# Causal attention: small masked tiles joined two to a PSUM bank, with a new order of jobs

## The chip, the cores and the metric

One core of one Trainium2 chip runs the kernel. The metric is the device time of one execution in microseconds (us); where several executions were timed, their median. Engines are named as in the profile: PE (TensorE matmuls), PEld (its weight loads), DVE (VectorE), ACT (ScalarE), POOL (GpSimd), SP (the DMA issuing queue).

## The reference

Two transformer layers on x of shape 4 x 1024 x 128, all in f32. Each layer normalises, attends with 16 heads of 8 dimensions, adds, normalises, applies a gated feed-forward network of 384 hidden units and adds. The second layer's attention is causal, and its projection weights are 8 times larger, so its scores spread widely and the softmax needs a true row maximum.

```python
logits = jnp.einsum('bshd,bkhd->bhsk', q, k) / np.sqrt(hd)
mask = k_pos > q_pos
logits = jnp.where(mask[None, None, :, :], -jnp.inf, logits)
attn = jax.nn.softmax(logits, axis=-1)
out = jnp.einsum('bhsk,bkhd->bshd', attn, v).reshape(b, s, d)
return out @ W_out + b_out
```

## The kernel before

A **window** is one sequence and four heads, so each layer has 16 windows. A window's queries fall into two halves of 512 (f = 0 or 1), each half into four blocks of 128 (qb).

For every window the kernel runs two passes over the scores. The first finds the row maxima. It is cut into **jobs**: one matmul of 128 queries against up to 512 keys into one PSUM bank (L1100), which DVE then reduces to a column of maxima, by a plain reduction where no key is masked (L882) and by a reduction with a mask added where the tile touches the diagonal (L879). In the causal layer a window has 48 tiles: 16 whole ones of 512 columns, and 32 masked ones, eight each of 128, 256, 384 and 512 columns. Before the change each tile is one job. Jobs take turns in a ring of three banks (`job_ring=3`): PE waits on `ring_free` before it writes a bank (L1095), DVE waits on `ring_full` before it reads one (L876).

When all jobs of a half are reduced, DVE negates the maxima (L888), POOL splits them in two bf16 parts (L536, L538), PE transposes them (L1150, the *shift* unit), ACT copies them and SP sends them by DMA into two spare rows of the query operand (L430). The second pass can then compute scores with the maximum already subtracted: a *scores* unit (L1132) holds two heads of one block of 128 keys, with up to 512 queries each, plus four small matmuls that add the mask on the diagonal (L1140). ACT takes the exponential (L653), a *sums* block on PE multiplies by the values (L1166), and at a half's end a *norm* unit transposes the sums (L1028). Scores units share a ring of two.

Heads 0 and 2 use array rows 0 to 63, heads 1 and 3 rows 64 to 127 (L1099, L1131), so that neighbouring matmuls of heads of different parity can run side by side. Sums blocks and shift units use 32-column tiles of the array instead.

Every engine walks one list, `Plan.walk` (L99 to L131), written as a string `order` for one **turn**: j is a job, s a scores unit, p a sums block, H and h shift units, N and n norm units. Turn t issues the scores and sums of window t; its jobs are those of later windows, `jobs_ahead` jobs further on. With 59 jobs ahead and 48 per window, the first scores of window 0 come after all 48 jobs of window 0 and 11 of window 1, and in turn 14 only 37 jobs are left. The list `tiles` gives the jobs' sequence within a window; a token such as `321` is head 3, block 2, key half 1. Each engine's program is in order, so a wait holds everything behind it.

The first jobs of the causal layer are issued during the end of the previous layer: 18 on PE (L1246, L1251, L1266, L1273) and 22 on DVE (L969, L984, L995), between the last feed-forward and projection work. DVE's `split_parts` there (L813) leads to the stores to DRAM and to the load of window 1's operands by SP (L421), which window 1's first job waits for (L1098).

Of the kernel before, what the change touches and what calls it, by code (L numbers as in the profile page):

```python
# [13 lines left out]
P = 128  # L14
# [36 lines left out]
class Plan:  # L51
# [12 lines left out]
    def __init__(self, causal, heads, unit_ring, job_ring, alternate, order, jobs_ahead, sums_behind, project_at, wide_step=99, tiles=None):  # L64
# [15 lines left out]
        for f in range(2):  # L80
            for qb in range(TPC):
                width = (TPC * f + qb + 1) * P if causal else S
                in_head_order = [(c, kh) for r in range(PAIRS) for kh in range(2) for c in (2 * r, 2 * r + 1)] if alternate \
                    else [(c, kh) for c in range(HG) for kh in range(2)]
                for c, kh in in_head_order:
                    w = min(width - kh * CHUNK, CHUNK)
                    if w > 0:
                        stream.append((f, c, qb, kh, w, causal and kh * CHUNK + w == width))
        if tiles:
            found = {x[:4]: x for x in stream}  # L90
            stream = [found.pop((f, *(int(d) for d in token))) for f in range(2) for token in tiles[f].split()]
            assert not found
        self.first_job = stream[0]
        self.last_of_half = [[x for x in stream if x[0] == f][-1] for f in range(2)]
# [53 lines left out]
    def ends_half(self, job):  # L148
# [8 lines left out]
              order="jjHjsjjsjjjspjssjjpjsjjsjspjjssjjpsjjpjssjjpjsjjsjpsjjjspjjssjjpjjsjspjjjhnNjjsjpjjssjjp",  # L157
              jobs_ahead=59, sums_behind=1, project_at=(4, 6, 10),
              tiles=("120 110 030 130 020 320 330 100 230 010 220 300 000 310 210 200",
                     "310 121 311 100 030 300 211 200 321 031 201 230 110 231 120 210 221 330 021 001 320 010 301 331 111 000 101 011 131 220 130 020"))]  # L160
# [7 lines left out]
def transformer_pair_kernel(nc, x_in, wqkv_a, bqkv_a, wout_a, bout_a, wqkv_b, bqkv_b, wout_b, bout_b,  # L168
# [10 lines left out]
    with ExitStack() as ctx:  # L179
# [590 lines left out]
        def _(dve):  # L770
# [95 lines left out]
            def run_job(layer, job, number):  # L866

                plan, job_base = PLANS[layer], layer * PLANS[0].jobs_all
                f, c, qb, kh, width, diagonal = job
                if number in plan.paired:  # L870
                    if kh == 0:
                        run_pair(plan, f, c, qb, number // 4 * 2 + c % 2)
                    return
                slot = number % plan.job_ring
                src, dst = psum[:, plan.job_bank + slot, 0:width], maxima[:, f, c, qb, kh:kh + 1]
                dve.wait_ge(ring_full, job_base + number + 1)  # L876
                if diagonal:
                    dve.sem_inc(begun, 1)
                    nc.vector.tensor_tensor_reduce(out=junk[:, slot, 0:width], in0=src, in1=mask[:, CHUNK - width:], scale=1.0,  # L879
                                                   scalar=LOWEST, op0=ALU.add, op1=ALU.max, accum_out=dst).then_inc(ring_free, 1)  # L880
                else:
                    nc.vector.tensor_reduce(dst, src, AX_X, ALU.max).then_inc(ring_free, 1)  # L882
# [8 lines left out]
            def jobs_and_negations(layer, items):  # L891

                for kind, w, number, what in items:
# [6 lines left out]
                    if kind == "job" and PLANS[layer].ends_half(what):  # L900
                        unnegated.append((what[0], number + 1))
# [103 lines left out]
        def _(pe):  # L1005
# [79 lines left out]
            def run_job(layer, w, job, number):  # L1085

                plan, job_base = PLANS[layer], layer * PLANS[0].jobs_all
                f, c, qb, kh, width, _ = job
                if number in plan.paired:
                    if number % 4 == 0:  # L1090
                        two_pairs(plan, f, c, qb, number // 2)
                    return
# [3 lines left out]
                if job == plan.first_job:  # L1096
                    earlier = layer * len(range(buf, WINDOWS, BUFS))
                    pe.wait_ge(operands_loaded[buf], (w // BUFS + earlier + 1) * LOADS)  # L1098
                rows, r = slice(TILE_ROWS * (c % 2), TILE_ROWS * (c % 2) + JOB_ROWS), c // 2  # L1099
                mm(psum[:, bank, 0:width], qop[rows, buf, f, r, qb * P:(qb + 1) * P].bitcast(F32R),  # L1100
                   kop[rows, buf, r, kh * CHUNK:kh * CHUNK + width].bitcast(F32R), start=True, stop=True).then_inc(ring_full, 1)
# [215 lines left out]
```

## Time and profile before

| what | value |
| --- | --- |
| median of 3 runs | 1334.71 us (1332.62 to 1335.34) |
| profiled execution | 1338.29 us, span 1336.4 us |
| mean granted clock of PE | 0.968 of full |
| causal attention, first to last exponential | 839.14 to 1270.41 us |
| one steady turn | 26.8 us |

The span runs from the first to the last instruction of the profiled execution; the execution's own time holds some 2 us besides. A matmul's recorded end is modelled and includes the time its result takes to leave the array, so PE looks busy almost throughout; the distance from one start to the next tells more. A turn begins with the exponential of its first scores unit.

### The profile page before, as it was taken

To read this page: it belongs to the slowest core of one execution; us is meant where nothing else is said; L and a number is where in the kernel's file an instruction comes from. 1 tells how busy PE (TensorE), PEld (TensorE's weight loads), DVE (VectorE), ACT (ScalarE), POOL (GpSimd) and SP (SyncE) were. 2 spreads that over 40 slices of the span, in tenths; PEclk is the share of its full clock that TensorE was granted. 3 is DMA by queue.
4 is the path that set the end of the run, shared out by engine and by line. 5 is a ranking of instruction groups with operands and counts; after the bars stand their busy time and mean duration, and the time that the engine had idled before them with its cause. 6 is when DMAs were issued, how large, how long until landed. Compare 5 with 4: busy or idle time off the path is not lost.

```text
span 1336.4 us, 26857 instructions
## 1 busy us (share of the span) xinstructions
PE 1290.7 (97%) x9681; PEld 656.2 (49%) x9681; DVE 1176.7 (88%) x2979; ACT 1004.5 (75%) x1791; POOL 142.1 (11%) x309
## 2 busy tenths in 40 slices
PE   8899999999999999999988987999999999999998
PEld 6434343433434443434335764555555555555487
DVE  7699999999999999999926988799899999999276
ACT  8678888888888888888884531677777777777753
POOL 5630000000000000000002211200000000000011
PEclk9689999999999999999999996799999999999999
DMA  7611001111101111100000433112111211120001
GB/s 209 204 33 34 21 14 34 33 33 34 32 8 29 34 33 33 33 23 13 2 1 1 122 99 95 34 39 59 36 35 38 59 37 34 35 64 4 3 25 40
DMA packets 40060, 58.44 MB, mean 44 GB/s; under 512 B 7796, under 2 KB 19448, under 8 KB 39928
## 3 DMA queue, kind: packets, MB, share of 16 engines
q1 hardware_dynamic: 39928, 56.72, 17.7%
q8 instruction: 77, 1.26, 0.4%
q14 instruction: 55, 0.45, 0.1%
HBM read 36.77 MB, written 18.87 MB: 42 GB/s over the span
## 4 chain that ended last, share of the span: by engine, by line
PE 88%; DVE 5%; ACT 3%; issue 2%; DMA 1%; SPq 0%; POOL 0%; DVEq 0%; ACTq 0%; POOLq 0%
PE psum L1166 30%; PE psum L1132 21%; PE psum L1100 21%; PE psum L1253 4%; PE psum L1028 3%; PE psum L1237 2%; ACT probs L653 2%; PE psum L1140 2%; PE psum L1039 1%; DVE maxima L882 1%; DVE hid L958 1%; PE psum L1182 1%; PE psum L1077 1%; PE psum L1013 1%; PE psum L1150 1%
## 5 line engine op out<-in xcount | busy, mean ns | idle before, releaser
L653 ACT ACTIVATE probs<-psum 128x512 f32<-128x512 f32 (+3 forms) x1386 | 821.8, 669 | 153.0 <-PE psum L1132 83.0
L882 DVE TENSOR_REDUCE maxima<-psum 128x1 f32<-128x512 f32 x1232 | 767.8, 682 | 8.6 <-PE psum L1100 6.6
L1100 PE MATMUL psum<-kop,qop 62*128 62x512 f32 (+2 forms) x1744 | 519.4, 429 | 7.0 <-DVE maxima L879 3.1
L1132 PE MATMUL psum<-qop,kop 64*128 64x512 f32 (+3 forms) x1792 | 514.2, 427 | 9.2 <-ACT probs L653 7.9
L1166 PE MATMUL psum<-probs,v 128*32 128x512 f32 (+3 forms) x3584 | 440.5, 564 | 0.7 <-ACT sums L660 0.7
L1100 PEld LDWEIGHTS psum<-kop,qop 62*128 62x128 f32 x1744 | 266.4, 189 | 203.4 <-DVE maxima L882 119.3
L1132 PEld LDWEIGHTS psum<-qop,kop 64*128 64x128 f32 x1792 | 247.5, 187 | 232.1 <-ACT probs L653 205.9
L879 DVE CUSTOM_DVE_ANT_0 junk<-psum,mask 128x512 bf16<-128x512 f32 (+3 forms) x512 | 232.6, 487 | 38.7 <-PE psum L1100 34.9
L1166 PEld LDWEIGHTS psum<-probs,v 128*32 128x32 f32 x3584 | 71.1, 108 | 120.0 <-issue 89.2
L546 POOL TENSOR_TENSOR att<-att_raw,rden 128x128 f32<-128x128 f32 x64 | 26.1, 409 | 536.9 <-DVE rden L911 536.9
L1140 PE MATMUL psum<-half_ident,key_mask 64*128 64x64 bf16 x1024 | 74.3, 197 | 0.0
L536 POOL TENSOR_TENSOR shift<-negmax,zeros 128x16 bf16<-128x16 f32 x64 | 14.2, 223 | 470.9 <-DVE negmax L888 462.5
L669 ACT CAST shift_rows<-psum 32x128 f32<-32x128 bf16 x64 | 16.5, 258 | 56.2 <-PE psum L1150 56.2
L1237 PE MATMUL psum<-ffn_xt,gate_up_w 128*128 128x512 f32 x192 | 52.6, 409 | 6.0 <-DVE hid L958 5.9
L793 DVE TENSOR_TENSOR x<-psum,x 128x512 f32<-128x512 f32 x32 | 22.1, 690 | 39.7 <-PE psum L1182 26.4
L1253 PE MATMUL psum<-down_w,hid 128*128 128x128 f32 x384 | 48.1, 282 | 4.8 <-DVE hid L958 4.7
L1140 PEld LDWEIGHTS psum<-half_ident,key_mask 64*128 64x128 bf16 x1024 | 43.2, 96 | 18.4 <-issue 6.5
L745 ACT ACTIVATE hid<-psum 128x512 f32<-128x512 f32 x48 | 28.5, 598 | 30.3 <-PE psum L1237 29.9
L1253 PEld LDWEIGHTS psum<-down_w,hid 128*128 128x128 f32 x384 | 45.3, 196 | 7.7 <-DVE hid L958 7.1
L620 ACT ACTIVATE qk<-psum,bqk 128x512 f32<-128x512 f32 x32 | 21.1, 684 | 32.8 <-PE psum L1039 32.6
L879 DVE DVE_READ_ACCUMULATOR2_ANT maxima<- 128x1 f32 x512 | 42.5, 83 | 0.0
L1028 PE MATMUL psum<-ident,sums 128*128 128x128 f32 x256 | 38.7, 283 | 2.4 <-ACT sums L660 1.6
(102 smaller groups left out, 750.4 us busy)
## 6 DMA issues: line engine op xcount, KB each, us to landing
qop<-q_parts SPq DMA_DIRECT2D x256, 64.0 KB
kop<-k_parts SPq DMA_DIRECT2D x64, 128.0 KB
kop<-k_parts SPq DMA_DIRECT2D x128, 64.0 KB
q_parts<-parts SPq DMA_DIRECT2D x24, 256.0 KB, 2.9
k_parts<-parts SPq DMA_DIRECT2D x24, 256.0 KB, 3.2
x<-in_L_attn_a_x SPq DMA_DIRECT2D x8, 256.0 KB, 4.6
q_parts<-att SPq DMA_DIRECT2D x8, 256.0 KB, 3.7
k_parts<-att SPq DMA_DIRECT2D x8, 256.0 KB, 3.8
```

Of the source, the lines that this page charges most:

```text
L546: nc.gpsimd.tensor_tensor(dst, att_raw[:, f, :, :, 0:HD], rden[:, f].rearrange("p t (h o) -> p t h o", o=1).broadcast_to([P, TPC, HG, HD]) ...
L653: nc.scalar.activation(probs[:, slot, heads[0] % 2:heads[-1] % 2 + 1, c0:], psum[:, bank:bank + len(heads), c0:], ACT.Exp, scale=SCORE_SCA ...
L745: nc.scalar.activation(hid[:, c, :], psum[:, 2 + 2 * (c % 2), :], ACT.Silu, scale=DEQUANT).then_inc(silu_ready, 1)
L879: nc.vector.tensor_tensor_reduce(out=junk[:, slot, 0:width], in0=src, in1=mask[:, CHUNK - width:], scale=1.0, scalar=LOWEST, op0=ALU.add, ...
L882: nc.vector.tensor_reduce(dst, src, AX_X, ALU.max).then_inc(ring_free, 1)
L1028: ins = nc.tensor.transpose(psum[:, bank, t * P:(t + 1) * P], src[:, t, :], ident[:])
L1100: mm(psum[:, bank, 0:width], qop[rows, buf, f, r, qb * P:(qb + 1) * P].bitcast(F32R), kop[rows, buf, r, kh * CHUNK:kh * CHUNK + width].bit ...
L1132: ins = mm(psum[:, bank + k, c0:], kop[rows, buf, c // 2, j * P:(j + 1) * P].bitcast(F32R), qop[rows, buf, f, c // 2, c0:].bitcast(F32R), ...
L1140: ins = mm(psum[:, bank + k, at:at + TILE_ROWS], key_mask[rows, part, :], half_ident[rows], start=False, stop=part == 1)
L1166: ins = mm(psum[32 * c:32 * c + 32, 7, c0:], v[:, at:at + 32], probs[:, slot, c % 2, c0:], start=(j == 0), stop=(s == plan.half_end[f]), t ...
L1237: ins = mm(psum[:, 2 + 2 * (c % 2) + k, :], gate_up_w[:, k, c, :].bitcast(F32R), ffn_xt[:, part].bitcast(F32R), start=part == 0, stop=part ...
L1253: ins = mm(psum[:, 7, t * P:(t + 1) * P], hid[:, c, t * P:(t + 1) * P], down_w[:, c, :], start=(c == 0), stop=(c == FB - 1))
```

## The change

A list token may now join tiles with a plus, and each entry of the list is one job of one or two tiles. The joined tiles are 128 with 384 columns or 256 with 256, so a job never exceeds one bank; their heads have the same parity. PE writes both tiles one behind the other into one bank and signals once; DVE waits once, reduces each tile with its own instruction as before and frees the bank once. Of the 48 tiles of a window 24 are joined, so that it has 36 jobs. The order of the turn, the tile list and the number of jobs ahead (59 to 37) are new. The counts of jobs issued early stay at 18 and 22.

```diff
--- before.py
+++ after.py
@@ -86,12 +86,15 @@
                     w = min(width - kh * CHUNK, CHUNK)
                     if w > 0:
                         stream.append((f, c, qb, kh, w, causal and kh * CHUNK + w == width))
+        stream = [(x,) for x in stream]
         if tiles:
-            found = {x[:4]: x for x in stream}
-            stream = [found.pop((f, *(int(d) for d in token))) for f in range(2) for token in tiles[f].split()]
+            found = {x[:4]: x for x, in stream}
+            stream = [tuple(found.pop((f, *(int(d) for d in tile))) for tile in token.split("+"))
+                      for f in range(2) for token in tiles[f].split()]
             assert not found
+            assert all(sum(x[4] for x in job) <= CHUNK and len({x[1] % 2 for x in job}) == 1 for job in stream)
         self.first_job = stream[0]
-        self.last_of_half = [[x for x in stream if x[0] == f][-1] for f in range(2)]
+        self.last_of_half = [[x for x in stream if x[0][0] == f][-1] for f in range(2)]
         units = [(s, h) for s in range(n) for h in heads]
         assert order.count("j") == len(stream) and order.count("s") == len(units) and order.count("p") == n
         ends = {"H": ("shift", 0, 1), "h": ("shift", 1, 0), "N": ("norm", 0, 0), "n": ("norm", -1, 1)}
@@ -154,10 +157,10 @@
               order="sjjsjpsjjjsspsjjsjspsjjsjspsjsjsjjsjssjjsjspHssjjsjpsjjsjspjjsjsspjsjssjsjjsnjsjjsspjssjsjpjssjsjpjssjsjpsjjsjspsjjsjspsjjsjsjsjsjsNhjjsjsspssjjjsps",
               jobs_ahead=48, sums_behind=2, project_at=(9, 11, 14), wide_step=5),
          Plan(causal=True, heads=PAIR_UNITS, unit_ring=2, job_ring=3, alternate=True,
-              order="jjHjsjjsjjjspjssjjpjsjjsjspjjssjjpsjjpjssjjpjsjjsjpsjjjspjjssjjpjjsjspjjjhnNjjsjpjjssjjp",
-              jobs_ahead=59, sums_behind=1, project_at=(4, 6, 10),
-              tiles=("120 110 030 130 020 320 330 100 230 010 220 300 000 310 210 200",
-                     "310 121 311 100 030 300 211 200 321 031 201 230 110 231 120 210 221 330 021 001 320 010 301 331 111 000 101 011 131 220 130 020"))]
+              order="jsjjsjHpjssjjsspjjjssppjsjsjpjjssjpjjsjspjjsjspjjsjspjjjhnNjsjjspjjsjspjjssp",
+              jobs_ahead=37, sums_behind=1, project_at=(4, 6, 10),
+              tiles=("230 130 330 000+020 200+220 110+310 010+210 300+320 030 100+120",
+                     "231 200 101+121 031 220 301+321 000 310 201+221 331 110 001+021 300 230 131 010 130 030 120 320 011+211 100 020 111+311 210 330"))]
 
 
 SHIFT_PAIR = 2 * -(-[item[0] for item in PLANS[0].walk].index("shift") // 4)
@@ -866,20 +869,25 @@
             def run_job(layer, job, number):
 
                 plan, job_base = PLANS[layer], layer * PLANS[0].jobs_all
-                f, c, qb, kh, width, diagonal = job
                 if number in plan.paired:
+                    f, c, qb, kh, _, _ = job[0]
                     if kh == 0:
                         run_pair(plan, f, c, qb, number // 4 * 2 + c % 2)
                     return
-                slot = number % plan.job_ring
-                src, dst = psum[:, plan.job_bank + slot, 0:width], maxima[:, f, c, qb, kh:kh + 1]
+                slot, column = number % plan.job_ring, 0
                 dve.wait_ge(ring_full, job_base + number + 1)
-                if diagonal:
+                if job[0][5]:
                     dve.sem_inc(begun, 1)
-                    nc.vector.tensor_tensor_reduce(out=junk[:, slot, 0:width], in0=src, in1=mask[:, CHUNK - width:], scale=1.0,
-                                                   scalar=LOWEST, op0=ALU.add, op1=ALU.max, accum_out=dst).then_inc(ring_free, 1)
-                else:
-                    nc.vector.tensor_reduce(dst, src, AX_X, ALU.max).then_inc(ring_free, 1)
+                for f, c, qb, kh, width, diagonal in job:
+                    src, dst = psum[:, plan.job_bank + slot, column:column + width], maxima[:, f, c, qb, kh:kh + 1]
+                    if diagonal:
+                        ins = nc.vector.tensor_tensor_reduce(out=junk[:, slot, column:column + width], in0=src,
+                                                             in1=mask[:, CHUNK - width:], scale=1.0, scalar=LOWEST,
+                                                             op0=ALU.add, op1=ALU.max, accum_out=dst)
+                    else:
+                        ins = nc.vector.tensor_reduce(dst, src, AX_X, ALU.max)
+                    column += width
+                ins.then_inc(ring_free, 1)
 
             def negate_max(layer, f, index):
 
@@ -898,7 +906,7 @@
                             negate_max(layer, f, jobs)
                         unnegated.clear()
                     if kind == "job" and PLANS[layer].ends_half(what):
-                        unnegated.append((what[0], number + 1))
+                        unnegated.append((what[0][0], number + 1))
 
             def causal_jobs(first, last):
                 jobs_and_negations(1, PLANS[1].walk[first:last])
@@ -1085,8 +1093,8 @@
             def run_job(layer, w, job, number):
 
                 plan, job_base = PLANS[layer], layer * PLANS[0].jobs_all
-                f, c, qb, kh, width, _ = job
                 if number in plan.paired:
+                    f, c, qb, _, _, _ = job[0]
                     if number % 4 == 0:
                         two_pairs(plan, f, c, qb, number // 2)
                     return
@@ -1096,9 +1104,13 @@
                 if job == plan.first_job:
                     earlier = layer * len(range(buf, WINDOWS, BUFS))
                     pe.wait_ge(operands_loaded[buf], (w // BUFS + earlier + 1) * LOADS)
-                rows, r = slice(TILE_ROWS * (c % 2), TILE_ROWS * (c % 2) + JOB_ROWS), c // 2
-                mm(psum[:, bank, 0:width], qop[rows, buf, f, r, qb * P:(qb + 1) * P].bitcast(F32R),
-                   kop[rows, buf, r, kh * CHUNK:kh * CHUNK + width].bitcast(F32R), start=True, stop=True).then_inc(ring_full, 1)
+                column = 0
+                for f, c, qb, kh, width, _ in job:
+                    rows, r = slice(TILE_ROWS * (c % 2), TILE_ROWS * (c % 2) + JOB_ROWS), c // 2
+                    ins = mm(psum[:, bank, column:column + width], qop[rows, buf, f, r, qb * P:(qb + 1) * P].bitcast(F32R),
+                             kop[rows, buf, r, kh * CHUNK:kh * CHUNK + width].bitcast(F32R), start=True, stop=True)
+                    column += width
+                ins.then_inc(ring_full, 1)
 
             def causal_jobs(first, last):
                 for _, w, number, job in PLANS[1].walk[first:last]:
```

## Rows read from the trace of the kernel before

**Rows 1.** The profile's page: the engines' busy line, then the granted clock in forty slices.
```profile
PE 1290.7 (97%) x9681; PEld 656.2 (49%) x9681; DVE 1176.7 (88%) x2979; ACT 1004.5 (75%) x1791; POOL 142.1 (11%) x309
...
PEclk9689999999999999999999996799999999999999
```

**Rows 2.** Stretches of the trace: first turn, thirteen steady turns, two last; us, busy (count) by engine, clock.
```profile
839.14:871.33 32.19, 32.19 (x255) 16.70 (x253) 24.52 (x82) 19.85 (x28) 3.47 (x6) 0.77 0.16 34
871.33:1220.18 348.85, 348.57 (x3461) 188.29 (x3461) 320.27 (x1093) 259.84 (x390) 21.00 (x78) 1.00 0.20 42
1220.18:1244.51 24.33, 24.21 (x254) 12.88 (x253) 18.93 (x58) 19.98 (x31) 1.61 (x6) 1.00 0.01 3
1244.51:1270.41 25.90, 22.69 (x230) 10.55 (x228) 4.26 (x16) 21.84 (x33) 2.08 (x4) 1.00 0.01 2
```

**Rows 3.** Timeline of ACT over one turn's wide stretch: start us, us, instructions.
```profile
985.47 2.85 ACT L653 ACTIVATE probs<-psum 128x1024 f32<-128x1024 f32 x3 [0.29 <-PE psum L1132]
...
988.73 5.96 ACT L653 ACTIVATE probs<-psum 128x1024 f32<-128x1024 f32 x6
995.05 1.73 ACT L653 ACTIVATE probs<-psum 128x1024 f32<-128x1024 f32 x2 [0.36 <-PE psum L1140]
```

**Rows 4.** Stretches: that wide stretch, and the rest of the same turn.
```profile
985.45:995.01 9.56, 9.54 (x84) 4.50 (x82) 8.41 (x23) 9.07 (x10) 0.00 (x0) 1.00 0.28 47
995.01:1012.22 17.21, 17.21 (x186) 9.94 (x185) 16.21 (x63) 10.91 (x20) 1.62 (x6) 1.00 0.17 38
```

**Rows 5.** Timeline of DVE in a wide stretch.
```profile
963.00 0.55 DVE L879 CUSTOM_DVE_ANT_0 junk<-psum,mask 128x384 bf16<-128x384 f32 x1
963.47 0.08 DVE L879 DVE_READ_ACCUMULATOR2_ANT maxima<- 128x1 f32 x1
...
964.05 1.29 DVE L882 TENSOR_REDUCE maxima<-psum 128x1 f32<-128x512 f32 x2
965.26 0.28 DVE L879 CUSTOM_DVE_ANT_0 junk<-psum,mask 128x128 bf16<-128x128 f32 x1
965.46 0.08 DVE L879 DVE_READ_ACCUMULATOR2_ANT maxima<- 128x1 f32 x1
966.37 0.69 DVE L879 CUSTOM_DVE_ANT_0 junk<-psum,mask 128x512 bf16<-128x512 f32 x1 [0.82 <-PE psum L1100]
966.98 0.08 DVE L879 DVE_READ_ACCUMULATOR2_ANT maxima<- 128x1 f32 x1
966.98 0.42 DVE L879 CUSTOM_DVE_ANT_0 junk<-psum,mask 128x256 bf16<-128x256 f32 x1
967.33 0.08 DVE L879 DVE_READ_ACCUMULATOR2_ANT maxima<- 128x1 f32 x1
```

**Rows 6.** Timeline of PE: single jobs, sums blocks and two jobs at once.
```profile
926.48 0.43 PE L1166 MATMUL psum<-probs,v 128*32 128x128 f32 x8
926.83 0.50 PE L1100 MATMUL psum<-kop,qop 62*128 62x512 f32 x1
...
927.60 0.48 PE L1100 MATMUL psum<-kop,qop 62*128 62x512 f32 x2
928.01 1.06 PE L1166 MATMUL psum<-probs,v 128*32 128x512 f32 x8
929.01 0.38 PE L1100 MATMUL psum<-kop,qop 62*128 62x256 f32 x1
```

**Rows 7.** Timeline of PE: two jobs of heads in one half of the array.
```profile
1002.97 0.59 PE L1100 MATMUL psum<-kop,qop 62*128 62x256 f32 x2
```

**Rows 8.** Timeline of DVE: two waits ahead of the causal layer.
```profile
798.42 0.69 DVE L879 CUSTOM_DVE_ANT_0 junk<-psum,mask 128x512 bf16<-128x512 f32 x1 [1.17 <-PE psum L1100]
...
811.54 0.69 DVE L804 TENSOR_TENSOR v<-psum,bvo 128x128 f32<-128x128 f32 x3 [2.40 <-PE psum L1041]
```

**Rows 9.** Timeline of PE: first job of window 1, first scores of window 0.
```profile
830.39 0.87 PE L1100 MATMUL psum<-kop,qop 62*128 62x384 f32 x3 [1.38 <-DMA kop<-k_parts]
...
837.47 1.00 PE L1132 MATMUL psum<-qop,kop 64*128 64x512 f32 x2
```

## The prediction

> **What bounds the kernel now.** I read the page first, for how busy the engines are and where PE's clock falls [rows 1]. Then I cut the causal attention into its turns [rows 2], since the change leaves everything else alone but for the 18 (PE) and 22 (DVE) jobs issued early. A steady turn takes 348.85 / 13 = 26.83 us. In it DVE is busy for 320.27 / 13 = 24.64 us, ACT for 19.99 us, and PE all the time by the record, which says little. The last turn, without jobs, takes 25.90 us with DVE nearly idle: there the dependence between ACT and PE sets the pace.
>
> One steady turn has two parts. In ACT's timeline [rows 3] ten wide exponentials of the second half (128x1024) begin from 985.47 on, the tenth at 995.05; six of them follow each other without a break. In this wide stretch ACT is busy 9.07 of 9.56 us and DVE 8.41 [rows 4]: ACT is the bound, and DVE starves now and then. In the other 17.21 us DVE is busy 16.21 us and ACT only 10.91 [rows 4]: there DVE, with PE close behind it, is the bound. DVE's largest wait of a turn lies in the wide stretch: after a 128-column tile it stands idle for 0.82 us until PE delivers the next job [rows 5]. PE was held by a sums block of 1.00 us (928.01 to 929.01 for such a block [rows 6]) and the scores behind it, and the three banks held 0.60 + 0.60 + 0.20 us of work for DVE. So a small tile costs a whole bank and gives DVE little to do while PE is away.
>
> **The change part by part.**
>
> *DVE's work.* Start to start, a masked tile takes 0.20 us at 128 columns, 0.35 at 256, 0.47 at 384 and 0.61 at 512; a whole one takes 1.21 / 2 = 0.60 [rows 5]. Eight of each masked width and 16 whole ones make 8 x 1.63 + 9.6 = 22.6 us; the change adds and removes none of these instructions. It removes 12 waits and 12 bank signals per turn, which I cost at nothing: back-to-back tiles show no idle time between them [rows 5]. DVE's floor for a turn stays 24.64 us.
>
> *The ring.* Each bank now holds 0.60 to 0.70 us of work (128 + 384: 0.67; 256 + 256: 0.70), three banks 1.8 us or more, where before the least was 0.20 + 0.35 + 0.61 or so. The holes in the new order (PE work between two jobs) are a sums block of at most 1.00 us with one or two scores units, and once two norm units with a shift. The 0.82 us hole should close.
>
> *The order.* I counted DVE's work between the first and the tenth wide scores unit in both orders, with the times above. Before, the jobs there sum to 7.7 us; after, to 8.8 us. ACT's time for the stretch stays 9.6 us, so 1.1 us of DVE work moves to where DVE was waiting, and the DVE-bound rest of 17.2 us loses as much: 26.83 - 1.1 = 25.7 us a turn. Both scores and exponentials keep their number and width.
>
> *PE.* A second way to the same figure. Sums blocks take 0.35 us at 128 columns and 1.00 at 512, start to start [rows 6], so (1.00 - 0.35) / 384 = 1.7 ns per column and 0.13 us fixed per block. The new order sets two sums blocks side by side once, and a shift next to a sums block once: 2 x 0.13 = 0.26 us less. Two 512-column jobs of heads in different halves of the array take 0.48 us together [rows 6] where one alone records 0.50. In the new order 8768 columns have such a neighbour against 7104; at (0.50 - 0.38) / 256 = 0.47 ns per column [rows 6] the extra 1664 save up to 0.8 us. Together up to 1.05 us: a PE-paced turn would take 25.8. I take 25.7 us.
>
> The first of these two terms rests on a fixed cost of each change between 32-column tiles and the wide ones. The Trainium skill ("TensorEngine Tiling (Array Packing)", Key Properties) says that changing the tiling mode drains the engine; the row agrees with a fixed part of 0.13 us, and by the rule alone the saving has the same sign.
>
> *Bounds of the turn.* Below, DVE's 24.64 us and some remainder: 24.8. Above, nothing regained: 26.83, and with the costs named under the rivals 27.3.
>
> *The start.* Before, the first scores begin at 837.47, 7.1 us after the first job of window 1, which had waited for its operands until 830.39 [rows 9]. Eleven jobs of window 1 and their two shifts stand between. Afterwards only two jobs of window 1 stand ahead of the scores, about 1.1 us at the low clock. But the early jobs are heavier: the first 22 now carry 32 tiles and 14.2 us of DVE work, not 9.8. Of these 4.4 us some lie in DVE's waits of 1.17 and 2.40 us [rows 8], the rest delays the last parts, their stores, and window 1's load. I take 2.5 us of delay (nearest: 4.4 less the part of the waits that is free) with bounds 0 and 4.4. The first scores then begin at 830.4 + 2.5 + 1.1 = 834.0: 3.5 us earlier; bounds 1.6 and 6. Seven tiles fewer lie ahead; they move into turn 14.
>
> *The turns.* Turn 0 runs partly at the low clock, 0.77 in the mean, and takes 32.19 us [rows 2]; it keeps this surplus and gains like the others. Turns 0 to 13 gain 14 x (26.83 - 25.7) = 15.8 us. Turn 14 took 24.33 us with 37 of 48 jobs [rows 2]; now it has 35 of 36 and takes a full 25.7: 1.4 us lost. Turn 15 has no jobs in either kernel, and keeps its 25.90 us within 1 us.
>
> *Other queues.* The shift DMAs and loads of SP follow the shift units. H now stands after the second scores unit instead of before the first, with six jobs and six scores units before the first scores that need it, and window w+2's first job comes at the turn's last job instead of the 38th of 48, so its load has more time. POOL is busy 1.6 us a turn. I cost these at nothing; if H's shift were late, PE would stand at its transpose and lose what it is late by.
>
> *Sum.* -3.5 - 15.8 + 1.4 = -17.9 us. The profiled execution took 1338.29 us (span 1336.4), the median is 3.6 us below it, and the difference is taken from the median: 1334.7 - 17.9 = 1316.8 us.
>
> **The rivals.**
>
> *DVE reaches its floor* (chance 0.13). If the ring never runs dry a turn takes 24.8 us: -3.5 - 28.4 + 0.5 = -31.4, so 1303 us. For it: small tiles stood in the ring ahead of the 0.82 us hole. Against: DVE still waits in the rest of the turn, PE's load there is high, and the norm hole stays.
>
> *Same-half serialisation* (0.09). The two tiles of a job always use the same half of the array. Two such jobs, 256 and 384 columns, take 0.59 us [rows 7] where two of 512 in different halves take 0.48 [rows 6]; at 0.47 ns per column the 128 columns of difference explain 0.06 of 384 against 256, and about 0.1 us is the second weight load in the open. Twelve a turn cost 1.2 us and eat the 1.1 us: 26.9 us a turn, 1334.7 + 0.1, no change. Against: adjacent pairs of the same half already exist, and in the whole turn they go down from 27 to 24. The Trainium skill ("TensorE: Matmul & The Clock Gate", Part 3: Packing small matmuls, The mechanism) says that a weight load overlaps a running matmul only when the row groups differ. The 0.59 us row agrees; by the rule the pairing speaks against this change, by the count of all neighbours it does not.
>
> *PE stands behind a full bank* (0.13, slower). A bank is now held 0.67 to 0.70 us where small tiles freed it after 0.20 or 0.35. In the wide stretch ACT is the bound, and a scores unit queued on PE behind a job that waits for its bank comes late. DVE's 8.8 us in 9.6 leave 0.8 us of room. If five of the ten wide units come 0.2 us late the stretch grows by 1.0 us, and if the rest gains back only half, a turn takes 27.3: -3.5 + 6.6 + 3.0 = +6.1, so 1341 us. It decides from 27.1 us a turn on. Against: ACT's waits in the stretch are now 0.29 and 0.36 us only, and the orders set a job or two at most between scores.
>
> *The forecast* has 0.65.
>
> **How the numbers follow.** A measurement here tells 0.2% (2.7 us) from no change. By the sum that is a turn below 26.7 us for faster and above 27.1 for slower. Forecast and floor make faster 0.78; the same-half case makes 0.09 of no change; the blocked bank 0.13 of slower. The range reaches from the floor case (1303) to a turn that gains nothing (14 x 0 + 2.5 - 3.5 = -1, 1334): it leaves out the slower case and little else, under 2 in 10.
>
> **What would show it.** DVE still has 768 tile reductions in the causal layer with the same durations; its idle time per turn falls from 2.2 us to about 1.1; its largest single wait in the wide stretch is below 0.4 us. Steady turns take 25.2 to 26.2 us. The first scores begin 2 to 5 us earlier, the wait for window 1's operands ends later than 830.4 and DVE waits before it. If turns take 26.8 or more, the forecast's main term is wrong: then either ACT's waits in the wide stretch have grown (the blocked bank), or PE's job matmuls stand further apart (the same half). If turns are right and the time is not, the start or the last two turns are mispriced.

## The result, and the profile after

The changed kernel takes 1320.92 us (median of 4 runs, 1320.3 to 1325.21), the kernel before 1333.74 us (4 runs): a ratio of 0.9909, 95% interval 0.9892 to 0.9926. That is 12.8 us faster, where 17.9 us were forecast. The profiled execution took 1321.39 us, its span is 1319.5 us. It lies 16.9 us under the profiled execution of before, which was 4.5 us above its kernel's median; where most of that came from is told below.

The page of the changed kernel, against [rows 1]:

```profile
PE 1270.7 (96%) x9681; PEld 648.6 (49%) x9681; DVE 1162.8 (88%) x2979; ACT 1002.3 (76%) x1791; POOL 142.6 (11%) x309
...
PEclk9689999999999999999998997699999999999999
```

The turns of the causal layer in the changed kernel, cut as in [rows 2] (first turn, thirteen steady ones, the last two; us, then busy time and count of PE, PEld, DVE, ACT, POOL, then PE's clock, DMA share, GB/s):

```profile
833.23:864.25 31.02, 30.92 (x257) 17.13 (x259) 24.65 (x87) 19.65 (x28) 9.95 (x6) 0.78 0.18 36
864.25:1201.51 337.26, 336.71 (x3460) 183.82 (x3460) 309.40 (x1093) 258.24 (x390) 21.41 (x78) 1.00 0.20 44
1201.51:1227.15 25.64, 25.60 (x265) 13.82 (x263) 23.11 (x82) 19.86 (x30) 1.79 (x7) 1.00 0.01 3
1227.15:1253.51 26.36, 22.31 (x231) 10.39 (x229) 4.26 (x16) 21.84 (x34) 2.52 (x6) 1.00 0.01 2
```

A steady turn takes 337.26 / 13 = 25.94 us, 0.89 less than before. Over thirteen turns that is 11.6 us of the 16.9. The first turn, counted from the first exponential, begins 5.9 us earlier (833.23 for 839.14) and takes 1.2 us less, the last two 1.3 and 0.5 us more. Behind the last exponential both profiles have 66.0 us left. Together these make up the 16.9 us.

The number that did not fit was DVE's. The prediction wanted its idle time to fall from 2.2 to about 1.1 us a turn; it stayed at 25.94 - 23.80 = 2.14. Instead its busy time fell from 24.64 to 309.40 / 13 = 23.80 us a turn although it executes the same reductions. One turn of the changed kernel, in the two parts of [rows 4]:

```profile
975.50:985.16 9.66, 9.66 (x79) 3.93 (x80) 8.92 (x30) 9.06 (x10) 0.28 (x2) 1.00 0.39 66
985.16:1001.42 16.26, 16.20 (x194) 10.09 (x187) 14.85 (x58) 10.81 (x21) 1.21 (x4) 1.00 0.11 28
```

The wide stretch has kept its length, 9.66 us for 9.56, as forecast. DVE is busy 8.92 us in it for 8.41, half of the 1.1 us more that were forecast. The rest took 16.26 us for 17.21, nearly the 1.1 us that were to go, but DVE's busy time there fell by 1.36 us. DVE's longest wait in this wide stretch is 0.42 us (0.83 before in the stretch of [rows 4]). Its longest of a turn, 0.6 us, now lies outside the wide stretch, as here ahead of 947.28; behind a sums block that began at 945.60, PE came to this job only at 946.60:

```profile
947.28 0.69 DVE L884 CUSTOM_DVE_ANT_0 junk<-psum,mask 128x512 bf16<-128x512 f32 x1 [0.61 <-PE psum L1110]
```

At the start of the causal layer the wait for window 1's operands has grown (PE waited 1.38 us for them before [rows 9]). DVE and PE stand still for 5.5 us until window 1's operands land:

```profile
822.04 4.25 PE L1110 MATMUL psum<-kop,qop 62*128 62x512 f32 x9
831.84 0.79 PE L1110 MATMUL psum<-kop,qop 62*128 62x512 f32 x2 [5.54 <-DMA kop<-k_parts]
832.40 0.66 PE L1144 MATMUL psum<-qop,kop 64*128 64x512 f32 x2
```

```profile
826.05 0.08 DVE L884 DVE_READ_ACCUMULATOR2_ANT maxima<- 128x1 f32 x1
...
832.79 0.69 DVE L884 CUSTOM_DVE_ANT_0 junk<-psum,mask 128x512 bf16<-128x512 f32 x1 [5.46 <-PE psum L1110]
```

### The profile page after: what moved, and what is told of

It reads as the page before. It is cut to its first block, busy times and chain, and to the rows that moved or that the text cites. A ratio compares the mean times of both kernels' runs of the same rounds, so it can differ in the third digit from the quotient of the medians.

```text
span 1319.5 us, 26665 instructions
## 1 busy us (share of the span) xinstructions
PE 1270.7 (96%) x9681; PEld 648.6 (49%) x9681; DVE 1162.8 (88%) x2979; ACT 1002.3 (76%) x1791; POOL 142.6 (11%) x309
## 4 chain that ended last, share of the span: by engine, by line
PE 88%; DVE 5%; ACT 3%; issue 2%; DMA 1%; POOL 1%; SPq 0%; DVEq 0%; POOLq 0%
PE psum L1178 30%; PE psum L1110 21%; PE psum L1144 20%; PE psum L1265 4%; PE psum L1036 3%; PE psum L1249 2%; PE psum L1152 2%; ACT probs L656 2%; DVE maxima L888 1%; PE psum L1047 1%; DVE hid L966 1%; PE psum L1194 1%; PE psum L1085 1%; PE psum L1021 1%; PE psum L1162 1%
## 5 line engine op out<-in xcount | busy, mean ns | idle before, releaser
L1110 PE MATMUL psum<-kop,qop 62*128 62x512 f32 (+2 forms) x1744 | 499.7, 426 | 9.8 <-DMA kop<-k_parts 5.5
L1144 PEld LDWEIGHTS psum<-qop,kop 64*128 64x128 f32 x1792 | 255.4, 188 | 213.4 <-ACT probs L656 186.2
L1110 PEld LDWEIGHTS psum<-kop,qop 62*128 62x128 f32 x1744 | 252.4, 189 | 214.8 <-DVE maxima L884 93.7
L884 DVE CUSTOM_DVE_ANT_0 junk<-psum,mask 128x384 bf16<-128x384 f32 (+3 forms) x512 | 222.3, 485 | 20.5 <-PE psum L1110 20.1
L1152 PE MATMUL psum<-half_ident,key_mask 64*128 64x64 bf16 x1024 | 83.2, 197 | 0.0
L1249 PEld LDWEIGHTS psum<-ffn_xt,gate_up_w 128*128 128x128 f32 x192 | 33.7, 189 | 14.7 <-DVE hid L966 8.4
```

What stands on the lines that cost most here:

```text
L884: ins = nc.vector.tensor_tensor_reduce(out=junk[:, slot, column:column + width], in0=src, in1=mask[:, CHUNK - width:], scale=1.0, scalar=L ...
L1110: ins = mm(psum[:, bank, column:column + width], qop[rows, buf, f, r, qb * P:(qb + 1) * P].bitcast(F32R), kop[rows, buf, r, kh * CHUNK:kh ...
L1144: ins = mm(psum[:, bank + k, c0:], kop[rows, buf, c // 2, j * P:(j + 1) * P].bitcast(F32R), qop[rows, buf, f, c // 2, c0:].bitcast(F32R), ...
L1152: ins = mm(psum[:, bank + k, at:at + TILE_ROWS], key_mask[rows, part, :], half_ident[rows], start=False, stop=part == 1)
L1249: ins = mm(psum[:, 2 + 2 * (c % 2) + k, :], gate_up_w[:, k, c, :].bitcast(F32R), ffn_xt[:, part].bitcast(F32R), start=part == 0, stop=part ...
```

## The experiments

**Pairing and order taken apart.** Two kernels carry one half of the change each. The first keeps the changed order and sequence of tiles and gives every tile its own bank:

```diff
-order="jsjjsjHpjssjjsspjjjssppj...", jobs_ahead=37
+order="jsjjjsjjHpjjssjjjjsspjjjjssppj...", jobs_ahead=49
-tiles=("230 130 330 000+020 200+220 ...
+tiles=("230 130 330 000 020 200 220 ...
```

> The changed kernel with its order and its sequence of tiles kept, but every tile a job of its own with a bank of its own (48 jobs a turn again, 49 ahead, the same tiles issued early). If the fuller banks shorten the turn, the ring runs dry again where small tiles stand in it, more so than in the kernel before, whose order was made for single tiles: steady turns of 26.8 to 28 us instead of 25.94, and the time 1335 us or more. If the new order alone does it (jobs moved into the wide stretch, blocks side by side), turns stay at 26.0 to 26.2 us and the time within 4 us of 1321.

The counts of early jobs are 26 and 32 in it, so that the same tiles go early. It took 1467.26 us (1.099 times the kernel before, 1.0911 to 1.1069). Its thirteen steady turns, and the first two of them by themselves:

```profile
883.77:1334.84 451.07, 406.44 (x3460) 208.40 (x3458) 320.21 (x1093) 267.05 (x391) 21.52 (x79) 0.91 0.16 33
883.77:916.03 32.26, 28.66 (x268) 14.90 (x266) 24.62 (x85) 20.52 (x31) 1.67 (x7) 1.00 0.18 35
916.03:955.75 39.72, 36.78 (x268) 17.94 (x266) 24.71 (x85) 20.61 (x31) 1.63 (x7) 0.74 0.12 28
```

They take 34.7 us each on average, in single turns 32.3 to 39.8. In the waits from 985.2 to 1024.03, which is one long turn and the 3 us ahead of it (who waited for whom, total us, times, longest), PE's weight loads wait for banks, and ACT behind them for scores:

```profile
ACT probs L656 <- PE psum L1152: 12.2, 12, 4.2
PEld psum L1110 <- DVE maxima L888: 8.8, 14, 0.9
DVE maxima L888 <- PE psum L1110: 8.0, 9, 2.3
```

The direction was that of the fuller banks, the size far beyond the 26.8 to 28 us expected. Two things add up. In the turns with the granted clock at 1.00 throughout, a turn takes 32.3 us, 6.3 more than in the changed kernel, and PE stands idle for 3.6 us of it (under 0.1 us in the changed kernel). In other turns the clock is at its lower level, 1.2 GHz, for a part of the turn; that makes the mean 34.7 us. One wait of ACT, 4.2 us, lies in such a part:

```profile
990.00:993.00 3.00, 2.97 (x37) 2.29 (x35) 2.59 (x15) 1.64 (x5) 0.00 (x0) 0.86 0.04 8
993.00:996.00 3.00, 3.00 (x17) 0.92 (x15) 0.39 (x2) 1.10 (x2) 0.00 (x0) 0.50 0.61 154
...
999.00:1002.00 3.00, 3.00 (x24) 1.64 (x16) 0.94 (x4) 1.31 (x3) 0.29 (x2) 0.50 0.34 57
1002.00:1005.00 3.00, 2.85 (x21) 1.11 (x21) 2.38 (x8) 2.78 (x4) 0.00 (x0) 0.94 0.00 0
```

The groups of small tiles that the order sets between two scores units need one, two or three banks when joined and up to four when not; the ring has three. So I read the 6.3 us as PE waiting for DVE in the middle of a group, with everything behind it in its queue; the waits above fit this, and no run with a fourth bank tests it. Ahead of the fall of the clock (at about 992) PE had stood idle for 0.3 to 0.6 us before several jobs. The clock then stayed at 1.2 GHz for some 10 us, and in the changed kernel, where PE has no such idle times, it is at 1.00 in all steady turns.

The second kernel has the old order and list, with 12 pairs joined at the place of their first tile (and 12 and 16 jobs issued early):

```diff
-order="jjHjsjjsjjjspjssjjpjs...", jobs_ahead=59, tiles=("120 110 030 130 020 320 ...
+order="HssjjjspjssjjpjsjjsjspjjssjjpsjjpssjjpsjjspsjjspssjjpjjsjspjjjhnNjjsjpjssjjp", jobs_ahead=46,
+tiles=("300+120 110+310 030 130 200+020 100+320 330 230 010+210 000+220", ...)
```

> The other half of the change by itself: the order and list of before with 12 pairs of tiles of a window joined, each at the place of its first tile, 46 jobs ahead. If fuller banks alone shorten the turn, it falls to 25.9 to 26.4 us. If PE's order paces it, which here has 6144 columns beside the other half (7104 before) and 26 changes of tile size (28 before), it stays at 26.6 to 27.2 us.

It took 1357.86 us (1.0163, 1.0138 to 1.0187), with turns of 366.50 / 13 = 28.19 us:

```profile
871.72:1238.22 366.50, 360.06 (x3460) 190.66 (x3460) 312.56 (x1093) 262.68 (x391) 21.00 (x78) 1.00 0.19 40
```

Neither theory had that: 1.36 us a turn more than before. DVE's idle time goes up from 2.2 to (366.50 - 312.56) / 13 = 4.15 us a turn, and its longest wait to 1.34 us:

```profile
974.69 0.69 DVE L884 CUSTOM_DVE_ANT_0 junk<-psum,mask 128x512 bf16<-128x512 f32 x1 [1.34 <-PE psum L1110]
```

So fuller banks alone are no gain in the old order. Why is argued only: a joined pair takes a job away from one place of the order, so PE has more other work between two jobs there, and its two tiles always use the same half of the array (32 neighbours of the same half in a turn, for 27 before).

**Which engine paces the turn.** Four kernels shorten one engine's work and leave the order alone. Each leaves out a part of the columns, so only its time is of use. The first two cut DVE's reductions, in the changed kernel and in the kernel before; the third cuts PE's jobs; in these three the exponential's scale is smaller too. The fourth cuts ACT's wide exponentials. In the diffs `wide` is the width less 128 for the whole causal tiles, and `c1` is 384 for the wide units of the second half.

```diff
-ins = nc.vector.tensor_reduce(dst, src, AX_X, ALU.max)
+ins = nc.vector.tensor_reduce(dst, src[:, 0:width - P * layer], AX_X, ALU.max)
```
```diff
-ins = mm(psum[:, bank, column:column + width], qop...
+ins = mm(psum[:, bank, column:column + wide], qop...
```
```diff
-nc.scalar.activation(probs[..., c0:], psum[..., c0:], ACT.Exp...
+nc.scalar.activation(probs[..., c0:c1], psum[..., c0:c1], ACT.Exp...
```

> The changed kernel with DVE's reduction of each whole causal tile taken over 384 of its 512 columns (and the causal exponential's scale divided by 100 so that it stays finite); 16 reductions a turn get 0.13 us shorter, 2.1 us in all. If DVE paces the turn, it falls from 25.94 by 1.5 to 2.1 us, to 23.8 to 24.4, and the time by 20 to 30 us. If PE or ACT paces it, the turn falls by less than 0.5 us.

> The same shortening of DVE's whole-tile reductions in the kernel before. If its turn of 26.83 was paced by DVE outside the wide stretch, it falls by 1 to 2 us. If it was paced by PE, which the ring held up, it falls by less than 0.5 us.

> The changed kernel with PE computing 384 of the 512 columns of each whole causal tile (DVE still reduces 512; scale divided by 100 as well): 16 x 128 columns less, 0.85 us a turn at 0.42 ns a column. If PE paces the turn, it falls by 0.5 to 0.85 us and the time by 8 to 13. If DVE does, by less than 0.3 us.

> The changed kernel with the exponential of each wide unit of the causal second half over 384 of 512 columns per head: ten of them a turn get some 0.21 us shorter, 2.1 us in all. If ACT bounds the wide stretch and the stretch bounds the turn, the stretch falls from 9.7 us to about 8 and the turn by 0.5 to 1.7 us. If DVE's work fills the turn whichever engine bounds a part, the stretch gets shorter, the rest longer and the turn falls by less than 0.3 us.

One execution each: 1320.59, 1331.34 (beside 1336.35 for the kernel before in the same series), 1313.71 and 1321.79 us. The thirteen steady turns, in this order:

```profile
864.03:1199.58 335.55, 334.99 (x3461) 180.54 (x3459) 286.36 (x1093) 258.32 (x390) 21.58 (x79) 1.00 0.21 44
```

```profile
864.84:1213.19 348.35, 348.20 (x3461) 183.51 (x3461) 295.07 (x1093) 259.79 (x391) 21.01 (x78) 1.00 0.20 42
```

```profile
862.55:1194.33 331.78, 331.24 (x3460) 184.62 (x3460) 309.13 (x1093) 258.07 (x391) 21.54 (x78) 1.00 0.21 44
```

```profile
867.79:1200.97 333.18, 332.64 (x3460) 184.30 (x3460) 309.48 (x1093) 231.77 (x390) 21.53 (x78) 1.00 0.21 44
```

How far such turns repeat is told by the runs below that leave the changed kernel's turn alone or nearly so: 25.92 to 25.95 us. DVE is busy 1.8 us less in a turn of the changed kernel, and the turn falls by 0.13 us, from 25.94 to 25.81. In the kernel before it is busy 1.9 us less, and the turn falls by 0.04 us, from 26.83 to 26.80. So DVE paced neither. Cutting PE's columns (0.85 us a turn by the expectation) gives 0.42 us, half of it; cutting 2.0 us of ACT's gives 0.31 us. Both lie between the two cases that were expected, and neither gives its full price.

The parts of a turn say the same. The first row is the rest of the turn in the kernel before with DVE's reductions shortened: 17.16 us, for 17.21 [rows 4], although DVE is busy only 15.34 us in it. The second is the wide stretch of the changed kernel with ACT's exponentials shortened: ACT has 1.8 us less to do, and the stretch falls by 0.45 us, from 9.66 to 9.21, where about 8 was expected if ACT bound it:

```profile
988.48:1005.64 17.16, 17.16 (x186) 9.99 (x186) 15.34 (x63) 10.89 (x20) 1.62 (x6) 1.00 0.17 38
```

```profile
977.84:987.05 9.21, 9.21 (x79) 3.98 (x80) 8.72 (x28) 7.24 (x10) 0.29 (x2) 1.00 0.41 65
```

I read this as a chain that passes through PE in most of the turn and through ACT in a part of the wide stretch; where the one hands over to the other was not measured.

**What made PE's turn shorter.** The first kernel puts a job between the units that the new order had set side by side:

```diff
-order="jsjjsjHpjssjjsspjjjssppjsjsj...
+order="jsjjsjHjpssjjsspjjjsspjpsjsj...
```

> The changed kernel with a job put between the two sums blocks that stand side by side and one between the shift unit and the sums block behind it, so that PE changes between 32-column tiles and wide ones 28 times a turn as before, not 24. If PE paces the turn and each pair of changes costs 0.13 us, the turn grows from 25.94 by 0.2 to 0.4 us and the time by 3 to 7. If PE had room, by less than 0.1 us a turn and 2 us.

It took 1330.86 us (0.9977, 0.9961 to 0.9993), and its turns 344.30 / 13 = 26.48 us:

```profile
865.17:1209.47 344.30, 344.17 (x3460) 183.18 (x3460) 310.65 (x1093) 259.78 (x390) 21.45 (x78) 1.00 0.20 43
```

With two jobs moved and four more changes of tile size a turn takes 0.54 us more, above the 0.2 to 0.4 us expected, and more than half of the 0.89 us is gone. In the changed kernel the units side by side look like this on PE:

```profile
943.12 0.23 PE L1162 MATMUL psum<-ident_bf,shift 128*32 128x128 bf16 x1
943.13 0.44 PE L1178 MATMUL psum<-probs,v 128*32 128x128 f32 x8
943.50 0.50 PE L1110 MATMUL psum<-kop,qop 62*128 62x256 f32 x2
...
947.82 0.86 PE L1178 MATMUL psum<-probs,v 128*32 128x128 f32 x16
948.61 0.49 PE L1110 MATMUL psum<-kop,qop 62*128 62x512 f32 x1
```

And so in the kernel with jobs between them:

```profile
945.68 0.23 PE L1162 MATMUL psum<-ident_bf,shift 128*32 128x128 bf16 x1
945.84 0.50 PE L1110 MATMUL psum<-kop,qop 62*128 62x256 f32 x2
946.27 0.43 PE L1178 MATMUL psum<-probs,v 128*32 128x128 f32 x8
946.63 0.33 PE L1144 MATMUL psum<-qop,kop 64*128 64x128 f32 x2
...
950.59 0.43 PE L1178 MATMUL psum<-probs,v 128*32 128x128 f32 x8
950.94 0.50 PE L1110 MATMUL psum<-kop,qop 62*128 62x512 f32 x1
951.37 0.64 PE L1178 MATMUL psum<-probs,v 128*32 128x256 f32 x8
951.94 0.50 PE L1144 MATMUL psum<-qop,kop 64*128 64x512 f32 x2
```

The shift unit and the sums block behind it start within 0.01 us of each other and take 0.38 us to the next job; apart they take 0.16 + 0.36. Two sums blocks, one of 128 columns and one of 256, run as one group of 16 and take 0.79 us; apart they take 0.35 + 0.57. That is 0.14 and 0.13 us, 0.27 together, as much as the prediction had for them. The other half of the 0.54 us is not located: the run also moves two jobs to other places, and with that the moments at which PE, DVE and ACT wait for each other.

Two more kernels exchange heads among tiles of equal width, so that nothing but the half of the array changes. What is counted is each place of the sequence where a job stands next to a matmul of the other half, with the columns of the narrower of the two. By the count of the expectations the kernel before has 7104 columns a turn, the changed one 8768, the first of these kernels 2752 and the second 10880. (That count leaves out one pair, the job ahead of the turn's first scores unit: 256 columns in the kernel before and 512 in the other three. With it the change brings 9280 for 7360, 1920 more and not 1664; the differences among the last three stay.)

```diff
-tiles=("230 130 330 000+020 200+220 110+310 ...
+tiles=("230 330 130 200+020 100+120 010+210 ...
```
```diff
-tiles=("230 130 330 000+020 200+220 110+310 ...
+tiles=("230 330 030 300+320 200+020 110+310 ...
```

> The changed kernel with heads exchanged among tiles of the same block and key half: widths, order and joins stay, but only 2752 instead of 8768 columns of jobs stand next to a matmul of the other half of the array. If PE's load paces the turn, at 0.47 ns a column it grows by up to 2.8 us, to 27 to 28.7 us, and the time by 15 to 40 us. If DVE and the ring pace it, the turn grows by less than 0.5 us and the time by less than 8.

> As the run with few such neighbours, the other way: 10880 columns of jobs next to a matmul of the other half instead of 8768. If PE's load paces the turn, it falls by up to 1.0 us and the time by up to 15 us, to 1306 to 1316. If DVE and the ring pace it, turn and time change by less than 0.2 us and 3 us.

```profile
867.14:1222.57 355.43, 354.87 (x3461) 200.00 (x3459) 314.06 (x1093) 259.36 (x391) 21.56 (x79) 1.00 0.20 41
```

```profile
864.45:1201.40 336.95, 336.50 (x3462) 184.60 (x3460) 309.48 (x1093) 258.31 (x390) 21.58 (x79) 1.00 0.20 44
```

With few such neighbours the turn is 355.43 / 13 = 27.34 us and the time 1343.93 (1.0075, 1.0057 to 1.0093); with most of them 25.92 us and 1321.49 (0.9904, 0.9886 to 0.9921). 6016 columns less cost 1.40 us, 0.23 ns a column, and 2112 more gain 0.02 us. Fewer such neighbours also means more of the same half (43 for 24), and the run cannot tell the two apart. PE's load matters where it grows, at half the price that I had taken, and from the changed list on there is nothing more to be had in this way. Between the kernel before and the changed one no run measures the price.

**The start.** The next kernel issues fewer jobs early, and keeps everything else:

```diff
-PE_JOBS_AHEAD, DVE_JOBS_AHEAD = 18, 22
+PE_JOBS_AHEAD, DVE_JOBS_AHEAD = 13, 15
-causal_jobs(9, 12) ... causal_jobs(12, 15) ... (15, 18) ... (18, 22)
+causal_jobs(7, 9) ... causal_jobs(9, 11) ... (11, 13) ... (13, 15)
```

> The changed kernel with 15 instead of 22 jobs issued early on DVE and 13 instead of 18 on PE, so that some 22 tiles instead of 32 stand among the last work of the first layer. If the heavier early jobs delay the last parts, their stores and window 1's operands, the last store is issued some 3 to 4 us earlier, window 1's first job starts at about 829 instead of 831.8, DVE's wait of 5.5 us before it closes to under 1 us, and the time falls by 2 to 3.5 us to about 1318. If that load is not what the first scores wait for, the time stays at 1321 within 1 us; steady turns stay at 25.9 in both cases.

It took 1313.73 us (0.9847, 0.9828 to 0.9865), 7.2 us less than the changed kernel, where 2 to 3.5 were expected, and with one other the fastest of those that do all the work. Its first turns, and the last of DVE's waits for window 1:

```profile
829.15:857.70 28.55, 28.45 (x257) 15.62 (x259) 24.34 (x87) 19.57 (x28) 9.97 (x6) 0.88 0.20 39
857.70:1194.97 337.27, 336.72 (x3460) 183.93 (x3460) 309.51 (x1093) 258.33 (x391) 21.52 (x78) 1.00 0.21 44
```

```profile
825.50 0.08 DVE L884 DVE_READ_ACCUMULATOR2_ANT maxima<- 128x1 f32 x1
...
828.71 0.69 DVE L884 CUSTOM_DVE_ANT_0 junk<-psum,mask 128x512 bf16<-128x512 f32 x1 [1.93 <-PE psum L1110]
```

The steady turn is unchanged, 25.94 us. The first turn begins at 829.15, 4.1 us earlier. The last store is issued 5.0 us earlier (813.63 for 818.67), and DVE's wait closed to 1.93 us and not under 1. The other gain, 2.5 us in the first turn, was not expected: it goes with PE's clock (0.88 in the mean against 0.78). That is no accident of the one profile: the four executions have mean clocks of 0.975 to 0.977, those of the changed kernel 0.968 to 0.972. Why the clock rises earlier is not shown.

> As the run with 15 jobs issued early, with 9 on DVE and 8 on PE (14 tiles). If the heavier early jobs are worth less than the wait for window 1's operands costs, the store is earlier still and the time falls by 1 to 3 us below that run's 1313.7. If DVE, now left with more tiles before window 1, becomes what the first scores wait for, the first scores come no earlier than 829 and the time stays or rises by 1 to 3 us.

With 8 and 9 early jobs, made in the same way, it took 1313.88 us (0.9839, 0.9825 to 0.9854): neither better nor worse. The last store is issued another 4.1 us earlier (809.56), but the first turn begins only 1.7 us earlier and takes 0.4 us more, so neither of the two cases expected came out:

```profile
827.49:856.48 28.99, 28.87 (x257) 16.05 (x259) 24.04 (x84) 19.57 (x28) 9.92 (x6) 0.85 0.20 39
```

> The changed kernel with 15 early jobs and the list with most neighbours of the other half. If the two act apart, turn 25.92 as in the list's own run and the start of the run with 15 early jobs: 1313 to 1314 us. The list's own run had first scores 2.8 us later and a first turn 2.6 us shorter; if that was a matter of when PE's clock rose and not of the list, nothing of it remains here.

With both the 15 early jobs and the other list it took 1316.34 us (0.9852, 0.9838 to 0.9867), above the 1313 to 1314 expected, with turns of 25.92 us. By the intervals that cannot be told from the run with 15 early jobs alone. Its first turn takes 28.66 us, for 28.55 there; nothing is left of a shorter first turn by the list.

## Why the prediction was right or wrong

**The sum.** Forecast -17.9 us, measured -12.8 by the medians and -16.9 between the two profiles. The range held it, and the direction was right. In the profiles' terms the turns gave 3.0 us less than forecast (12.8 for 15.8), the start 2.4 us more and the last two turns 0.4 us less, so two errors of opposite sign made -16.9 come out near -17.9; that is luck. The further 4.1 us down to the medians is scatter between executions, told under the start and the first turn.

**The turn.** Forecast 25.7 us, measured 25.94. The size was nearly right and the first of its two derivations was wrong. The step that failed reads "so 1.1 us of DVE work moves to where DVE was waiting, and the DVE-bound rest of 17.2 us loses as much". The rest was not bound by DVE: the runs with shorter reductions leave the turn where it was, before the change as after. DVE's busy share of 94% there [rows 4] misled me. A reduction's record lasts 0.69 us while the next can start after 0.61 [rows 5], so a wait of under 0.08 us ahead of each tile is recorded as busy time; that is how I read the fall of DVE's busy time by 0.84 us with the same instructions, and it is why 24.64 us was never a floor (the prediction's own count of start-to-start times for the tiles came to 22.6 us). This reading of the records is argued from the rows, not tested by a run of its own. The premise that ACT bounds the wide stretch was right in part at most: 1.8 us less of ACT's work shortened it by 0.45 us.

**PE's two terms** point the right way, and neither is fully measured. Setting the units side by side was worth 0.54 us (forecast 0.26), of which PE's rows show 0.27 for the units themselves. The columns beside the other half of the array cost 0.23 ns each where they are taken away; at that price 1664 columns would be 0.4 us (forecast up to 0.8), and the 1920 of the full count 0.4 as well, but no run measures the price in this range, and above it 2112 columns more gave 0.02 us. That the two add up to about 0.9 or 1.0 us, against 0.89 observed, is therefore no proof. The rule of the Trainium skill ("TensorEngine Tiling (Array Packing)", Key Properties), that a change of tiling mode drains the engine, fits the 0.27 us that four such changes cost in the rows; the drain itself is not seen.

**The ring.** The 0.82 us hole is gone, but DVE's idle time of a turn is not (2.14 us for 2.2), so that is not where the time came from. The pairing is needed all the same: the new order without it takes 146 us more than with it. Neither the pairing nor the order is a gain by itself. As I read it, the pairing lets PE do four small tiles between two scores units without waiting for DVE, and the gain is then made by the order.

**The start** was forecast at -3.5 us. By the profiles the first scores come 5.1 us earlier (832.40 for 837.47) and the first turn begins 5.9 us earlier, of which 1.0 us had been gained before the first causal job in either kernel's code (793.12 for 794.08). Part of this is luck of the execution: two of the kernels above, the one with shorter exponentials and the one with jobs put between the units, do the same work as the changed kernel until then, and their first turns begin at 836.87 and 836.26, 2.3 and 2.9 us earlier than before. The heavier early jobs delayed the last store by 2.9 us (818.67 for 815.73), 3.9 us against the first job; I had taken 2.5, within bounds of 0 and 4.4. The wait this made, 5.5 us of both engines, stood in the prediction as a sign to look for and not as what it was, the largest thing found here that was left to gain. One count was wrong without harm to the sum: the kernel before has 14 jobs of window 1 ahead of the first scores and not 11, since its order sets three more jobs ahead of them (PE's rows from 830.39 to 837.47 have 14), and so 12 tiles fewer lie ahead now and not seven.

**The last turns**: turn 14 lost 1.3 us (forecast 1.4). Turn 15 lost 0.5 us (forecast none).

**The first turn** accounts for most of the 4.5 us by which the profiled execution of before stood above its median. In the thirteen profiles other than that of the kernel without pairs it takes either 28.2 to 29.2 us at a mean clock of 0.85 to 0.91, or 30.9 to 32.4 us at 0.77 to 0.80. The kernel before shows 32.19 in its own profile, and 28.55 in the profile of the run with shorter reductions, whose DVE work there cannot account for 3.6 us, as its steady turns show. Thirteen further executions of the kernel before go from 1330.78 us at a mean clock of 0.974 to 1338.27 at 0.968. What decides when the clock rises stays open.

**The rivals.** The floor for DVE fell with the theory that DVE sets one. Same-half serialisation did not eat the gain here; the list has fewer such neighbours than before (24 for 27), and the run with 43 of them takes 1.40 us a turn more. A blocked PE did not show in the changed kernel, whose PE is idle under 0.1 us a turn; by its idle time of 3.6 us it is what happened in the run without pairs.

## What to carry to other kernels

An engine that is busy 94% of a stretch need not pace it: shorten its work in one run and see whether the stretch follows, before building on it. Where several engines hand work to each other in order, what a small ring of banks can do depends on the work in each bank and on the order together: try both, since here neither change was a gain alone. When jobs get heavier, the counts that say how many of them go ahead of a critical transfer must be set anew; here that gave 7.2 us, more than half of what the change itself gave. And compare profiles by their steady turns, which repeat within 0.03 us here, before their starts, which do not.

## What was not expected of the hardware

Four more changes of PE between 32-column tiles and wide ones take 0.27 us in PE's rows, and the turn grew by 0.54 us in the one run that adds them. PE's many waits for banks in the run without pairs were followed by a fall of its clock from the upper to the lower level (0.50 of full speed for some 10 us in the stretch shown) in the middle of the layer, and the waits then grew. And the first turn of the causal layer takes 28.55 us in one execution and 32.19 in another, at mean clocks of 0.89 and 0.77, of two kernels whose steady turns agree within 0.04 us. That is 0.3% of this kernel's time and limits how finely its runs can be compared.
